# A state-space block on one core: softplus's polynomial product moves to GpSimd, GpSimd's input products move to other places, and the tile loops are written out

## The reference, cut to what matters

```
dt = softplus(einsum(dt, dt_proj_w) + dt_proj_b)      # 256 inner channels
A  = -exp(A_log)                                      # 256 x 16 states
def step(h, inp):
    dt_t, B_t, C_t, x_t = inp
    dA = exp(dt_t[:, :, None] * A)
    h  = dA * h + (dt_t * x_t)[:, :, None] * B_t[:, None, :]
    y  = einsum('bds,bs->bd', h, C_t)
    return h, y
y = ys + xc * D_param
y = y * silu(z)
return einsum('bld,od->blo', y, out_proj_w)
```

## Time and profile before

| | |
|---|---|
| median of 3 runs | 16619.03 us (16615.55 to 16625.17) |
| the profiled execution's own time | 16605.28 us |
| its span | 16603.5 us |
| DVE busy | 15104.1 us, 91% |
| POOL busy | 15002.7 us, 90% |
| PE busy | 14390.7 us, 87% |
| ACT busy | 11266.2 us, 68% |
| instructions | 158027 |

### The profile page before, as it was taken

The page is one execution under the profiler, slowest core; times in us unless marked ns, Lnnn a source line. Parts: engine busy times, 40 slices in busy tenths (PEclk is TensorE's granted clock), DMA queues, the critical chain, the costliest instruction groups (busy, mean ns, idle before and its releaser), DMA issues. The chain is left out here.

```text
span 16603.5 us, 158027 instructions
## 1 busy us (share of the span) xinstructions
PE 14390.7 (87%) x30720; PEld 5782.7 (35%) x30720; DVE 15104.1 (91%) x13023; ACT 11266.2 (68%) x18635; POOL 15002.7 (90%) x6275
## 2 busy tenths in 40 slices
PE   6888888888888888888888888888888888888888
PEld 2333333333333333333333333333333333333333
DVE  6999999999999999999999999999999999998988
ACT  5666667666666666666677666667666676667675
POOL 5999889998899989998899998999989999899998
PEclk9999999999999999999999999999999999999999
DMA  3444444444444444444444444444444444444443
GB/s 132 155 154 161 150 152 154 155 157 150 154 154 153 163 145 153 156 154 159 142 155 160 152 160 143 156 156 158 155 143 156 156 157 158 146 148 158 150 151 135
DMA packets 738975, 2535.44 MB, mean 153 GB/s; under 512 B 77240, under 2 KB 78016, under 8 KB 721728
## 3 DMA queue, kind: packets, MB, share of 16 engines
q1 hardware_dynamic: 738112, 2527.45, 44.8%
HBM read 2376.15 MB, written 150.99 MB: 152 GB/s over the span
## 5 line engine op out<-in xcount | busy, mean ns | idle before, releaser
L1467 POOL TENSOR_TENSOR RING<-RING,CS 128x1024 f32<-128x1024 f32 x4096 | 9833.9, 2416 | 1369.6 <-DVE RING L1148 1350.2
L1148 DVE TENSOR_TENSOR_SCAN RING<-DA,HS,RING 128x512 f32<-128x512 f32 x8192 | 9955.4, 1264 | 811.0 <-ACT DA L777 614.1
L388 PE MATMUL YP<-RING,EYE 128*128 128x512 f32 x16384 | 8293.4, 638 | 1648.6 <-POOL RING L1467 1578.7
L777 ACT ACTIVATE DA<-ITEM,AN 128x512 f32<-128x512 f32 x8192 | 5519.4, 685 | 3384.9 <-DVE RING L1148 3376.5
L388 PEld LDWEIGHTS YP<-RING,EYE 128*128 128x128 f32 x16384 | 3133.4, 199 | 6324.9 <-issue 3616.5
L1128 DVE TENSOR_TENSOR RING<-DTP,BS 128x1024 f32<-128x1024 f32 x2816 | 3375.5, 1206 | 0.4 <-DMA BS<-bc_rows 0.3
L1454 POOL TENSOR_TENSOR RING<-ITEM,BS 128x1024 f32<-128x1024 f32 x1280 | 3016.6, 2357 | 9.4
L388 PE MATMUL FL<-XN,WC 128*128 128x512 f32 x4096 | 1943.3, 618 | 9.7 <-ACT XN L864 4.6
L388 PEld LDWEIGHTS FL<-XN,WC 128*128 128x128 f32 x4096 | 839.4, 205 | 1129.8 <-issue 1121.5
L791 ACT ACTIVATE ITEM<-FL,COL 128x512 f32<-128x512 f32 x512 | 347.6, 679 | 1183.1 <-PE FL L388 1183.1
L388 PE MATMUL FL<-LS,WP 128*128 128x512 f32 x2048 | 995.6, 610 | 35.3 <-DVE XR L1184 29.2
(11 more groups left out here) (123 smaller groups left out, 10636.4 us busy)
## 6 DMA issues: line engine op xcount, KB each, us to landing
BS<-bc_rows SPq DMA_DIRECT2D x2048, 512.0 KB, 4.9
CS<-bc_rows SPq DMA_DIRECT2D x2048, 512.0 KB, 3.6
XR<-in_x SPq DMA_DIRECT2D x128, 1024.0 KB, 7.3
x_slices<-XR SPq DMA_DIRECT2D x64, 1024.0 KB, 8.1
XR<-x_slices SPq DMA_DIRECT2D x64, 1024.0 KB, 7.5
out<-XR SPq DMA_DIRECT2D x64, 1024.0 KB, 8.2
XR<-in_wqkv SPq DMA_DIRECT2D x24, 1024.0 KB, 7.3
bc_rows<-ROWS SPq DMA_DIRECT2D x256, 64.0 KB, 4.6
```

Of the source, the lines that this page charges most:

```text
L388: return pe.matmul(*a, **k)
L777: act.activation(DA[:, h, :], DT[:, i % 2, h, :], ACT.Exp, scale=AN[:, h, s:s + 1]).then_inc(dA_ready, 1)
L1148: dve.tensor_tensor_scan(H[:, slot(n), h, :], DA[:, h, :], U[:, slot(n), h, :], HS[:, i % ITEMS, h, s:s + 1], ALU.mult, ALU.add).then_inc( ...
L1467: pool.tensor_tensor(G[:, slot(n)], H[:, slot(n)], CS[:, s % C_ROWS, :].unsqueeze(1).broadcast_to([P, NH, T]), ALU.mult).then_inc(g_ready, 1)
```

## The change

It does four things.

1. `dt_poly` is split. ACT squares as before and then adds 13/16 by a second activation on the same tile (line 841 of the changed kernel, semaphore `factor_ready`); POOL multiplies by EM (line 1471), at step 10 + d between G and `dt_sum`.
2. `POOL_U` goes from (0, 1, 2, 7, 8) to (1, 7, 8, 10). DVE makes twelve u in place of eleven: 0 and 2 come to it and 10 leaves it.
3. `AHEAD` and `AHEAD_LATE` are moved: each u of DVE stands mostly a scan ahead, and u of state 0 (written 16) is made at step 15 of the window before.
4. The loops over tiles inside an image are written out on PE, ACT, DVE, POOL and SP. The loop over images stays.

```
-POOL_U = (0, 1, 2, 7, 8)
+POOL_U = (1, 7, 8, 10)
-AHEAD = ((), (), (3,), (4, 5), (6,), (), (), (9,), (10,), (11,), (12,), (13,), (14,), (15,), (), ())
+AHEAD = ((2,), (3,), (), (4,), (5, 6,), (), (), (9,), (), (11,), (12,), (13,), (14,), (15,), (), (16,))
-AHEAD_LATE = ((), (), (3,), (4,), (5, 6), (), (), (9,), (10,), ...
+AHEAD_LATE = ((2,), (3,), (), (4,), (5,), (6,), (), (9,), (), ...
...
                 act.activation(YZ[:, :, :], EM[:, :, :], ACT.Square, bias=CUBE_SHIFT, scale=CUBE).then_inc(square_ready, 1)
+                act.wait_ge(square_ready, tile * ITEMS + i + 1)
+                act.activation(YZ[:, :, :], YZ[:, :, :], ACT.Identity, bias=CUBE_REST).then_inc(factor_ready, 1)
...
-            def dt_poly(tile, i):
-
-                dve.wait_ge(square_ready, tile * ITEMS + i + 1)
-                dve.scalar_tensor_tensor(out=YZ[:, :, :], in0=YZ[:, :, :], scalar=13.0 / 16, in1=EM[:, :, :],
-                                         op0=ALU.add, op1=ALU.mult).then_inc(poly_ready, 1)
...
-                    if front:
-                        if s == 10 + d:
-                            dt_poly(tile, w + 1)
...
+            def dt_poly(tile, i):
+                pool.wait_ge(factor_ready, tile * ITEMS + i + 1)
+                pool.tensor_tensor(YZ[:, :, :], YZ[:, :, :], EM[:, :, :], ALU.mult).then_inc(poly_ready, 1)
...
                         if s == 10 + d:
+                            dt_poly(tile, w + 1)
                             dt_sum(tile, w + 1)
...
-                with dve.Fori(0, 4) as t:
+                for t in range(4):
                     for w in range(2, 2 + ITEMS):
                         window(b * NT + t, w, stat=(b + 1, t) if w == 3 else None)
```

More of the change, by code:

```diff
@@ L111, in block_ssm_kernel @@
         SKIP, EPSC, BV16, PBF = COL[:, 30:31], COL[:, 31:32], COL[:, 32:36], COL[:, 36:40]
-        NSMALL, ONESMALL, CUBE_SHIFT, ZERO, NLOGSMALL, LOGSMALL = (COL[:, n:n + 1] for n in range(40, 46))
+        NSMALL, ONESMALL, CUBE_SHIFT, ZERO, NLOGSMALL, LOGSMALL, CUBE_REST = (COL[:, n:n + 1] for n in range(40, 47))
         Q, K = QK[:, 0], QK[:, 1]
@@ L327, in image @@
                 tile_step(b, 0, tile, after_store=(b - 1, NT - 1) if b else None, stats=early(0))
-                with sp.Fori(1, 4) as t:
+                for t in range(1, 4):
                     tile_step(b, t, tile + t, after_store=(b, t - 1), stats=early(t))
-                with sp.Fori(4, 6) as t:
+                for t in range(4, 6):
                     tile_step(b, t, tile + t, after_store=(b, t - 1), stats=pair(t))
@@ L750, in _ @@
             with pe.Fori(0, BATCH - 1) as b:
-                with pe.Fori(0, NT - 2) as t:
+                for t in range(NT - 2):
                     for w in range(2, 2 + ITEMS):
@@ L759, in _ @@
             b = BATCH - 1
-            with pe.Fori(0, NT - 1) as t:
+            for t in range(NT - 1):
                 for w in range(2, 2 + ITEMS):
@@ L1094, in _ @@
             with act.Fori(0, BATCH - 1) as b:
-                with act.Fori(0, NT - 2) as t:
+                for t in range(NT - 2):
                     for w in range(2, 2 + ITEMS):
@@ L1106, in _ @@
             b = BATCH - 1
-            with act.Fori(0, NT - 1) as t:
+            for t in range(NT - 1):
                 for w in range(2, 2 + ITEMS):
@@ L1212, in window @@
                     n = w * NS + s
-                    make_ahead(tile, n, d, first=first)
+                    make_ahead(tile, n, d, first=first, front=front)
                     scan(tile, n, first=first)
@@ L1373, in first_front @@
                 scale_norm(tile + 1)
-                dt_poly(tile, 0)
                 dve.wait_ge(state_zeroed, image + 1)
@@ L1419, in _ @@
             first_front(0, 0)
+            make_u(0, 0, first=True)
             window(0, 0, first=True, ln2=False)
@@ L1422, in _ @@
             with dve.Fori(0, BATCH - 1) as b:
-                with dve.Fori(0, 4) as t:
+                for t in range(4):
                     for w in range(2, 2 + ITEMS):
                         window(b * NT + t, w, stat=(b + 1, t) if w == 3 else None)
-                with dve.Fori(4, 6) as t:
+                for t in range(4, 6):
                     for w in range(2, 2 + ITEMS):
@@ L1434, in _ @@
             b = BATCH - 1
-            with dve.Fori(0, NT - 1) as t:
+            for t in range(NT - 1):
                 for w in range(2, 2 + ITEMS):
@@ L1516, in _ @@
             dt_first(0, 0)
+            dt_poly(0, 0)
             dt_sum(0, 0)
@@ L1524, in _ @@
             with pool.Fori(0, BATCH - 1) as b:
-                with pool.Fori(0, NT - 1) as t:
+                for t in range(NT - 1):
                     for w in range(2, 2 + ITEMS):
```

16 lines of the change are left out of this document (9 added, 7 removed).

## The result

The changed kernel takes 16497.11 us (median of 4, 16491.02 to 16503.99) against 16621.56 us for the kernel before on the same chip (4 runs): ratio 0.9927, 95% interval 0.9915 to 0.9939. It is 0.73% faster, inside the range, but 200 us behind the 16300 of the forecast: two fifths of the gain came.

A forecast was written before the change was run, and what follows sets the result against it. A closed path through POOL and DVE was taken as the bound: four windows walked at 240.7 us a tile, 244.3 with allowance, against 250.1. Gains of 104, 88, 81 and 41 sum to 314 us, giving 16300, range 16150 to 16440.

The forecast's parts named there:

- Poly off DVE: DVE loses 2.1 us of busy time per window, and POOL's G, no longer held by the poly, 1.0 per window.
- Poly onto POOL: With u 10 to POOL and u 0, 2 to DVE, POOL keeps 24 products a window; busy POOL 14770, DVE 14850 us.
- the closed path: Loop from POOL's G 4 through `dt_x`, ACT's handover and DVE's scans to the next G 4: 58.4 us per plain window.
- ACT's second activation at nothing: ACT's added `Identity` takes 1.13 us but was costed at nothing; uncovered, it would be 290 us in all.
- Handover 1.8: From the end of POOL's `dt_x`, by ACT's copy and an `Exp`, to DVE's scan of state 14: 1.8 us.
- `gate`, u, scans: DVE's waits: `gate` for PE from 497 to under 150 us, scans for u gone, for dA 614 to 900-1200.
- Window 3: I take half of it, 1.8: Half of DVE's 3.57 us wait for ACT at step 5 stays, 1.8, making the window 60.3 us.
- the allowance of 0.9: Added to every window for the walk coming out some 0.5 short and for busy PE in window 1: 240.7 becomes 244.3.
- Window 2: +3.0, 61.4: Layer norm on DVE twice and two short ACT operations, less a later u, add 3.0 us: 61.4.
- Windows 0 and 1: `normalise` (4.5 us) makes window 0 59.9 us; an addition of 3.7 makes window 1 59.1.
- slower, dtx comes late: POOL's new work ahead of `dt_x` delays ACT's copy and scan 14; 2.31 us more per window, 16850 us; chance 0.10.
- TensorE or ACT takes what is given: Windows 1 and 3 stay, 0 and 2 gain; a tile gains 3 instead of 5.8: about 16450 us; chance 0.14.

The follow-up runs named there:

- e3: The changed kernel with the old `POOL_U`, `AHEAD` and `AHEAD_LATE`, so the poly on POOL and nothing taken off it: 16934.89 us, 1.0192.
- e6: The changed kernel with POOL's `dt_x` one G later (step 12 + d): 17030.19 us, 1.0243 to the kernel before.
- e2: The changed kernel with the poly back on DVE as one instruction and without ACT's second activation; loops written out and new tables kept: 16428.47 us, 0.9884.
- e18: e17 with the poly on DVE: 16232.91 us, 0.9779 to the kernel before.
- e17: e16 with TensorE's z matmuls of window 3 early as well: 16044.44 us, 0.9662 to the kernel before.
- e15: The changed kernel without ACT's second activation, so 13/16 is missing from the cubic: 16498.12 us, 0.9934 to the kernel before.
- e11: The changed kernel with window 3's z matmuls on TensorE in step 2, ahead of the `state_sum` that waits for `gate`: 16356.51 us, 0.9851.
- e16: The changed kernel with ACT's copy of dtx one step later, behind dA of state 14: 16140.82 us, 0.9715 to the kernel before.
- e5: The changed kernel with POOL's `dt_x` one G earlier (step 10 + d): 16372.43 us, 0.9849 to the kernel before.
- e7: The changed kernel with POOL making the u of state 2 in place of that of state 10, DVE the other way: 16433.54 us, 0.9885.
- e10: e2 with `dt_x` one G earlier: 16403.17 us, 0.9872 to the kernel before.
- e19: e17 with `dt_x` one G earlier: 16225.84 us, 0.9769 to the kernel before.
- e14: The changed kernel with its product made by DVE as a plain product, ACT's second activation kept: 16505.7 us, 0.9941 to the kernel before.
- e1: The kernel before with the tile loops written out and nothing else: 16584.74 us, 0.998.

## Why the prediction was right in direction and wrong in size

- **Poly off DVE:** right. G 2363 ns, DVE 14790 us. The price of holding each other, 1.0 per window, is near what POOL lost: (2416 - 2363) x 16 = 0.85.
- **Poly onto POOL:** the closed path has its price. One product more ahead of `dt_x` costs 350 us (e3) and 533 (e6). That the table had to take something off POOL was right too. Not foreseen was that the poly's move is the losing half of the change in this order of ACT: loops 30 won, tables 156 won, and then poly 70 lost, if they are taken in this order. By the Trainium skill (GPSIMD Engine Reference, section 4.1 Engine selection) elementwise work belongs on VectorE. e2 against the changed kernel agrees by 70 us; e18 against e17 goes the other way by 188. The rule's factor of two is in the rows (2368 ns against 1196 at least), but beside POOL's products the same work takes DVE 3030 ns in the mean (e2), and which engine the path runs through decides the rest.
- **ACT's second activation at nothing:** right with the product on POOL (e15). The sign that was to speak against it, waits for ACT at steps 8 to 11, did appear: 3.2 us a tile in the last image where there were 0.7. But e15 shows the same 3.2, so they come from elsewhere.
- **Handover 1.8:** right in windows 0 and 1 (1.8 in the rows above, and 1.9 and 1.8 in the mean).
- **`gate`, u, scans:** right. `gate` 63 us (under 150 forecast), no wait for u, scans 1152 (900 to 1200 forecast). POOL's idle time was to lie before G 4; in the rows above it lies before G of state 1 (0.98) and not there.
- **"Window 3: I take half of it, 1.8":** the step that failed most. The wait did not halve but went from 3.57 to 4.11. I had it that ACT is late behind TensorE, which is late behind POOL. That lateness did go: ACT's waits for PE at line 791 fell from 1183 to 111 us in the waits of the two kernels. But another took its place at line 797, from 25.5 to 213 us: TensorE is now late behind `gate`, in front of matmuls that do not need it. e11 settles this. From G 4 to G 4, window 3 takes 64.1 in the mean of the last image's tiles, not 60.3, and 61.2 in e11. Before, by the same tally, windows 0 to 3 took 62.6, 60.6, 60.5 and 66.2. So, with the allowance of 0.9, window 3 was to give 5.0 of what a tile was to gain; it gave 2.1. Windows 0 and 1 gave 1.3 and 0.6 (1.8 and 0.6 expected).
- **"Window 2: +3.0, 61.4":** 63.8, the second error in size. It is 3.3 longer than before, where 1.8 was expected. G 4 to the end of `dt_x` is 34.8, not 32.9: DVE waits in the loaded part for PE's mean of layer norm, and POOL then for DVE. DVE and POOL in the window 2 at 15105:

```profile
15114.39 2.29 DVE L1167 TENSOR_TENSOR LV<-LV,FL 128x2048 f32<-128x2048 f32 x1 [1.36 <-PE FL L388]
```

```profile
15120.33 2.37 POOL L1462 TENSOR_TENSOR RING<-RING,CS 128x1024 f32<-128x1024 f32 x1 [3.02 <-DVE RING L1151]
```

  I had POOL as the slower engine throughout this part. It idled 3.02 us in it.
- **Windows 0 and 1:** 61.3 and 59.9 for 59.9 and 59.1, from the mixed path read above. Together the four windows are 8.4 over the walk (249.1 against 240.7, by the same tally), and the allowance held 3.6 of these. It had been taken from one stretch, not from each kind of window.
- **Loops:** 30 to 35 us, counted as nothing. They worked towards more gain, so the windows fell short by more than the total shows. Tile 6 gained 6.8 (5.8 forecast) and tiles 4 and 5 4.1 each (6.3); the others 0.3 to 1.1 instead of 3.7 to 5.8.
- **The rival "slower, dtx comes late"** named the place: ACT in the copy holds back dA of state 14. e3 and e6 are this rival, and e16 shows that the changed kernel paid for it in every window. What I missed is that half of the way to it was already walked, and that it could be taken out.
- **The rival "TensorE or ACT takes what is given"** has the number nearest to the result, 16450, at a chance of 0.14. Its first half is true of window 3, where TensorE's order took what the change gave. But it had windows 1 and 3 unchanged and a gain in 0 and 2, while 0, 1 and 3 gained and 2 lost, and ACT's added operation took nothing (e15). That its time came close is in part luck.

## What to carry to other kernels

Where two engines hand work to each other in a ring, walk the ring once per kind of window and measure the walk on the kernel before, kind by kind, before using it on the kernel after; a shared allowance hides the windows in which a third engine decides. Look at every instruction that waits on an in-order engine and ask whether those queued behind it need the same thing: two such places, one on ACT and one on PE, were worth 2.7% here (e17 against the changed kernel), against 0.7% for the change itself. Whether a piece of work pays on another engine is not a property of the work: the same poly cost 70 us before these waits were gone and brought 188 after. And a path that was shown by making it longer (e3, e6) is not thereby a forecast of what making it shorter brings (e5, e7, e10, e19).

## What the runs showed of the hardware

- A DVE operation with both inputs in SBUF can be held far beyond its own length by back-to-back products on POOL: 1196 ns at least, 2426 in the median, 7142 at most in e2, and 3339 in the mean as a plain product (e14). The Trainium skill (SBUF — State Buffer, section Who interferes with whom) calls the ports that the two share an exclusive lock. The trace agrees in that the poly of the rows of e2 stands still to the end of a POOL product, and in that G takes 3.26 us and no longer 2.35 where the poly began first. It also shows that the poly can miss two changes from one POOL product to the next.
- After a pause of 5.26 us TensorE's first four matmuls took 3.76 us at a granted clock of 0.50, and the next four 1.90 at 0.99 (changed kernel, window 3 at 15149).
- A turn of a hardware loop over tiles, on five engines at once, cost about 0.6 us: some 30 us in about fifty turns (e1).
